# A message-passing kernel: every value product in the second pass, stores on SyncE, the two gathers in turn

## Chip, cores, metric

The kernel runs on 1 core of a Trainium2 chip. The metric is device time in microseconds of one execution. Three timed runs of the kernel before gave a median of 889.56 us (888.55 to 889.84).

## What is computed

A graph layer on N = 625 nodes and E = 20000 edges of F = 256 features, followed by a mixture-of-experts layer. Only the graph layer is touched by the change. Cut to what matters:

```
h    = concat([x[dst], x[src], edge_attr], axis=1)          # x layer-normalised, 20000 x 768
gate = sigmoid(bn(silu(h @ W1f + b1f) @ W2f + b2f))          # bn: mean and variance over all edges
msg  = gate * (silu(h @ W1m + b1m) @ W2m + b2m)
agg  = segment_sum(msg, dst, 625)                            # dst is sorted
x    = x + relu(x_ln + bn(agg)); then x + mixture_of_experts(layernorm(x))
```

`silu(h @ W1m + b1m)` is called the hidden value below, its product with W2m the value product, and `silu(h @ W1f + b1f) @ W2f` the gate product.

## The kernel before

The work is cut into stages that follow one another. Matrix products are done in three passes of rounded parts: each operand is split into a high part (`hi`, rounded) and the remainder (`lo`), and hi x hi, hi x lo and lo x hi are summed (`PASSES`). A product of two 128-row blocks of depth and 512 edges is thus six matmuls, and one of 256 x 256 with 512 edges is twelve.

**Setup (0 to about 36 us).** The node part of the first layer is computed once per node, into two tables in memory, `table_dst` and `table_src`, of 625 rows of 512 numbers each. SyncE stores them in pieces (L182, L187).

**Edge pass (to about 542 us).** Edges are taken in 40 groups of 512 (the last has 32), four groups (`b` = 0 to 3) to a turn of a hardware loop; group g is 4i + b. The batch normalisation of the gate needs statistics over all edges, so the gate can't be applied yet: the pass writes two intermediate arrays to memory, `z_gate` (gate product) and `h_val`. For each group:
- GpSimd gathers rows of the two tables by indirect DMA, four transfers of 128 rows for `dst` into `pre` (L122) and four for `src` into `from_src` (L404). There are four buffers; those of group g are free when TensorE has done group g-4 (`h1_psum`). VectorE adds the two (L512).
- SyncE loads the edge features `ea` (L117), TensorE transposes them (L555), ScalarE rounds (L417), VectorE makes the remainder (L488).
- TensorE does the first layer in four column blocks of six matmuls (L568), and adds the rows from `pre` by four transposing matmuls each (L577). Blocks 0 and 1 belong to the gate, 2 and 3 to the hidden value.
- ScalarE applies SiLU to the gate blocks twice (rounded, L450, and full, L451); VectorE makes the remainder (L531); TensorE does the gate product (L604), ScalarE copies it (L425) and issues the store of `z_gate` (L429), and VectorE takes its statistics (L494).
- Odd groups: ScalarE applies SiLU to the hidden value (L469) and issues its store to `h_val` (L433).
- Even groups: ScalarE makes the hidden value twice (L468, L469), VectorE its remainder (L525), TensorE the value product in the middle of the next, odd group's step (`value_layer`, L589), ScalarE adds the bias (L461) and issues the store of the finished value to `h_val` (L437).

**Message pass (about 542 to 734 us).** Per group the arrays are loaded again by SyncE (L319, L322; four buffers), ScalarE applies the sigmoid (L716), the message is gate times value, TensorE transposes it (L849), ScalarE rounds (L728), VectorE makes the remainder (L799), and TensorE adds it to the nodes by products with a one-hot matrix (L863), one window of 125 nodes at a time. VectorE makes the one-hot matrix of the next group with one operation for each window that the group touches (L791); which windows those are is read from a table, and the others are branched over.
- Even groups: `h_val` holds the finished value, and GpSimd makes the message for both halves in one operation (L692).
- Odd groups: `h_val` holds the hidden value. ScalarE rounds it (`hidden_hi`, L328), GpSimd makes the remainder (`split_hidden`, L332), TensorE does the value product (`second_layer`, L834), its half 0 one step before its half 1, and VectorE makes the message with the bias (L780). There are two message buffers.

**The rest (about 734 to 890 us)** is batch normalisation of the sums and the expert layer.

The order on each engine is written out by hand; engines meet only at semaphores, and a wait holds up everything that stands behind it on its engine.

## Time and profile before

The profiled execution took 891.85 us; its span from the first to the last instruction was 890.0 us, with a mean granted TensorE clock of 0.954. The page of the profile gives the busy time of each engine over that span:

| engine | busy us | share | instructions |
|---|---|---|---|
| TensorE (PE) matmuls | 801.7 | 90% | 4536 |
| TensorE (PEld) weight loads | 680.6 | 76% | 4537 |
| VectorE (DVE) | 538.2 | 60% | 883 |
| ScalarE (ACT) | 477.9 | 54% | 855 |
| GpSimd (POOL) | 451.4 | 51% | 391 |
| DMA | 226 GB/s over the span | | 67756 packets |

Matmuls are pipelined, so their durations overlap and the start of one to the start of the next is what it costs. An indirect DMA on GpSimd is counted as busy while its list of transfers is written.

### The profile page before, as it was taken

What the parts mean: (1) busy time and instruction counts of PE and PEld (TensorE: products, weight loads), DVE (VectorE), ACT (ScalarE), POOL (GpSimd) and SP (SyncE); (2) the same over time, 40 slices, a digit from 0 to 9 for tenths busy, and PEclk for the clock granted to TensorE, in tenths of its full rate; (3) what the DMA queues carried; (4) which work ended last, traced back from release to release, by engine and by line L of the source; (5) the groups of instructions that cost most, each with busy time, mean ns of one, the idle gap of its engine ahead of it and who ended that gap; (6) DMA issues with size and microseconds to landing.
All of it is one profiled execution on the core that took longest, in us unless ns stands there. A gap on an engine that the chain in (4) does not pass through costs nothing. (4 is left out here: it accounts for less than half of the span.)

```text
span 890.0 us, 14611 instructions
## 1 busy us (share of the span) xinstructions
PE 801.7 (90%) x4536; PEld 680.6 (76%) x4537; DVE 538.2 (60%) x883; ACT 477.9 (54%) x855; POOL 451.4 (51%) x391
## 2 busy tenths in 40 slices
PE   4579999999999999999999997888779874799998
PEld 3468888888888888888888885666667662799998
DVE  5257655566655555565665543888787874666664
ACT  4135555555555555555555555666557661565661
POOL 2578777666766667666666103556455573100000
PEclk9779999999999999999999996999999995699999
DMA  7778899888888878888889823676575733001201
GB/s 210 238 246 295 290 321 328 317 304 303 295 289 304 297 274 298 297 306 305 302 280 325 328 94 154 227 256 216 184 260 197 265 132 108 1 25 51 91 24 30
DMA packets 67756, 201.74 MB, mean 227 GB/s; under 512 B 10912, under 2 KB 18878, under 8 KB 67726
## 3 DMA queue, kind: packets, MB, share of 16 engines
q0 software_dynamic: 25024, 81.94, 28.3%
q1 hardware_dynamic: 31182, 77.48, 24.8%
q10 hardware_dynamic: 11520, 41.95, 12.3%
q8 instruction: 16, 0.26, 0.1%
q14 instruction: 14, 0.11, 0.0%
HBM read 156.19 MB, written 45.14 MB: 226 GB/s over the span
## 5 line engine op out<-in xcount | busy, mean ns | idle before, releaser
L122 POOL DMA_INDIRECT pre<-table_dst,idx x157 | 159.9, 1019 | 108.2 <-PE p_h L577 56.5
L404 POOL DMA_INDIRECT from_src<-table_src,idx x157 | 162.0, 1032 | 47.9 <-issue 47.9
L568 PE MATMUL p_h<-eaT_hi,w_hi 128*128 128x512 f32 (+1 forms) x320 | 134.4, 420 | 1.7 <-DVE eaT_lo L488 1.7
L568 PE MATMUL p_h<-eaT_lo,w_hi 128*128 128x512 f32 (+1 forms) x320 | 126.2, 394 | 0.0
L568 PE MATMUL p_h<-eaT_hi,w_lo 128*128 128x512 f32 (+1 forms) x320 | 125.8, 393 | 0.0
L494 DVE BATCH_NORM_STATS2 gate_stats<-zg_st 128x512 f32 (+2 forms) x80 | 54.3, 681 | 105.1 <-ACT zg_st L425 104.7
L531 DVE TENSOR_TENSOR h_lo<-h_full,h_hi 128x512 fp32r<-128x512 f32 (+1 forms) x80 | 54.5, 681 | 103.8 <-ACT h_full L451 103.5
L512 DVE TENSOR_TENSOR pre<-pre,from_src 128x512 f32<-128x512 f32 (+1 forms) x157 | 98.6, 688 | 11.9 <-DMA from_src<-table_src,idx 11.9
L577 PE MATMUL p_h<-ident,pre 128*128 128x128 f32 x628 | 95.4, 274 | 11.4 <-DVE pre L512 11.4
L577 PEld LDWEIGHTS p_h<-ident,pre 128*128 128x128 f32 x628 | 78.5, 141 | 33.8 <-DVE pre L512 12.1
L450 ACT ACTIVATE h_hi<-p_h 128x512 fp32r<-128x512 f32 (+1 forms) x80 | 47.1, 588 | 94.9 <-PE p_h L577 94.9
L692 POOL TENSOR_TENSOR msgT<-hv,gate 128x1024 f32<-128x1024 f32 x20 | 47.7, 2385 | 78.4 <-ACT gate L716 78.4
L863 PEld LDWEIGHTS p_agg<-msg,onehot 128*125 128x125 f32 x346 | 45.3, 193 | 46.1 <-DVE msg L799 45.8
L863 PE MATMUL p_agg<-msg,onehot 128*125 128x256 f32 x346 | 53.0, 299 | 30.1 <-DVE msg L799 30.1
L332 POOL TENSOR_TENSOR hvT_lo<-hv,hvT_hi 128x1024 fp32r<-128x1024 f32 x20 | 54.6, 2731 | 46.5 <-ACT hvT_hi L328 46.5
L791 DVE TENSOR_TENSOR onehot<-node_id,idx_num 128x500 fp32r<-128x500 f32 (+1 forms) x44 | 70.5, 1609 | 7.5 <-issue 6.9
L425 ACT COPY zg_st<-p_z 128x512 f32<-128x512 f32 (+1 forms) x80 | 46.1, 578 | 52.6 <-PE p_z L604 52.6
L469 ACT ACTIVATE hv_st<-p_h 128x512 f32<-128x512 f32 (+1 forms) x80 | 46.8, 586 | 46.2 <-PE p_h L577 46.1
L568 PEld LDWEIGHTS p_h<-eaT_hi,w_lo 128*128 128x128 f32 x320 | 60.6, 189 | 13.9
L568 PEld LDWEIGHTS p_h<-eaT_hi,w_hi 128*128 128x128 f32 x320 | 60.8, 190 | 11.8 <-issue 1.9
L568 PEld LDWEIGHTS p_h<-eaT_lo,w_hi 128*128 128x128 f32 x320 | 61.2, 191 | 9.3
L728 ACT CAST msg<-p_msg 128x512 fp32r<-128x512 f32 (+1 forms) x80 | 42.5, 580 | 48.2 <-PE p_msg L849 48.2
(213 smaller groups left out, 1876.9 us busy)
## 6 DMA issues: line engine op xcount, KB each, us to landing
z_gate<-zg_st ACTq DMA_DIRECT2D x40, 512.0 KB, 4.4
h_val<-hv_st ACTq DMA_DIRECT2D x40, 512.0 KB, 6.0
hv<-h_val SPq DMA_DIRECT2D x40, 512.0 KB, 5.5
gate<-z_gate SPq DMA_DIRECT2D x40, 512.0 KB, 4.6
ea<-in_edge_attr_dram SPq DMA_DIRECT2D x39, 512.0 KB, 6.9
raw<-in_L_ffn_W_dram SPq DMA_DIRECT2D x16, 512.0 KB, 4.6
pre<-table_dst,idx POOLq DMA_INDIRECT x157, 4.0
from_src<-table_src,idx POOLq DMA_INDIRECT x157, 5.8
```

What stands on the lines that cost most here:

```text
L122: pool.indirect_dma_start(pre[b][0:n, t, :], None, table_dst, bass.IndirectOffsetOnAxis(ap=idx[b][0:n, t:t + 1], axis=0)).then_inc(got_dst ...
L332: nc.gpsimd.tensor_tensor(hvT_hl[b // 2][1][:], hv[b][:], hvT_hl[b // 2][0][:], ALU.subtract).then_inc(hv_lo, 1)
L404: pool.indirect_dma_start(from_src[b][0:n, t, :], None, table_src, bass.IndirectOffsetOnAxis(ap=idx[b][0:n, T + t:T + t + 1], axis=0)).the ...
L450: nc.scalar.activation(h_hl[0][:, k, 0:w], p_h1[k][:, 0:w], ACT.Silu)
L494: nc.vector.bn_stats(gate_stats[:, j, bass.ds(g * 6, 6)], zg_st[par][:, j, 0:w]).then_inc(zg_stats, 1)
L512: nc.vector.tensor_tensor(pre[b][0:n, t, :], pre[b][0:n, t, :], from_src[b][0:n, t, :], ALU.add).then_inc(summed_ok, 1)
L531: nc.vector.tensor_tensor(h_hl[1][:, k, 0:w], h_full[k][:, 0:w], h_hl[0][:, k, 0:w], ALU.subtract).then_inc(h_lo_ok, 1)
L568: nc.tensor.matmul(p_h1[c][:, 0:w], w1_hl[wp][:, k, c * P:(c + 1) * P], eaT_hl[b % 2][dp][:, k, 0:w], start=n == 0, stop=False)
L577: last = nc.tensor.matmul(p_h1[c][:, t * TE:t * TE + n], pre[b][0:n, t, c * P:(c + 1) * P], ident[0:n, 0:n], start=False, stop=t == len(ro ...
L692: nc.gpsimd.tensor_tensor(msgT[0][:], hv[b][:], gate[b][:], ALU.mult).then_inc(msgT_even, 1)
L791: nc.vector.tensor_tensor(onehot[par][0:rows, 0:nt, n * TP:(n + 1) * TP], ids, dsts, ALU.is_equal)
L863: nc.tensor.matmul(p_agg[n // 2][:, n % 2, :], onehot[b % 2][0:rows, t, n * TP:(n + 1) * TP], msg[0:rows, part, t, :], start=False, stop=F ...
```

## The change

- `value_layer`, the second SiLU of even groups (L468), the remainder L525, the biased copy L461 and their semaphores go from the edge pass. `h_val` holds the hidden value for every group.
- The stores of `z_gate` and `h_val` are issued by SyncE, in the same queue as the loads of `ea`, instead of by ScalarE.
- Setup issues destination gathers for group 0 only; from then on each step of GpSimd issues the destination gathers of a group and then its source gathers. Before, setup issued destination gathers for groups 0 and 1, and groups 0 and 1 had only their source gathers in the loop.
- In the message pass every group is treated as the odd ones were: ScalarE `hidden_hi` and GpSimd `split_hidden` two groups ahead, TensorE the whole value product of the next group after the transposes of this one, VectorE both halves of the message. GpSimd's `message` goes, there is one message buffer, the sigmoid is done one group ahead instead of two, and VectorE makes the one-hot matrix after the two half messages.

```diff
@@ setup, GpSimd
-                    for b in range(2):
-                        gather_dst(pool, b)
+                    gather_dst(pool, 0)
@@ both passes
-            nc.scalar.copy(hvT_hl[b // 2][0][:], hv[b][:]).then_inc(hv_hi, 1)
+            nc.scalar.copy(hvT_hl[b % 2][0][:], hv[b][:]).then_inc(hv_hi, 1)
@@ edge pass, SyncE
+                    def store_gates(i, b, g):
+                        sp.wait_ge(zg_copied, KF * g + KF)
+                        sp.dma_start(z_gate[g], zg_st[b % 2][:]).then_inc(zg_stored[b % 2], 16)
+
                     def step(i, b, first=False, last=False):
                         g = 4 * i + b
                         if not (last and b >= 2):
                             sp.wait_ge(eaT_psum, KF * g + KF)
                             load_ea(sp, g + 2, b % 2, last and b == 1)
+                        if not (first and b == 0):
+                            store_gates(i, b + 1, g - 1)
+                        sp.wait_ge(hv_ok, KF * g + KF)
+                        sp.dma_start(h_val[g], hv_st[b % 2][:]).then_inc(hv_stored[b % 2], 16)
@@ edge pass, GpSimd
-                        if not (first and b < 2):
+                        if not (first and b == 0):
...
-                    for b in (1, 3):
-                        split_hidden(pool, 0, b)
+                    for b in range(2):
+                        split_hidden(pool, b, b)
@@ edge pass, ScalarE
-                        if not (first and b == 0):
-                            store_gates(g - 1, (b + 1) % 2)
-                            if b % 2 == 0:
-                                store_hidden(g - 1)
...
-                        if b % 2:
-                            for j in range(KF):
-                                act.wait_ge(v_made, KF * (2 * i + b // 2) + j + 1)
-                                nc.scalar.activation(hv_st[0][:, j, :], p_z[j][:, 0:G], ACT.Identity,
-                                                     bias=vecs[:, 3, j:j + 1]).then_inc(v_copied, 1)
...
-                            if b % 2 == 0:
-                                nc.scalar.activation(hvT_hl[1][0][:, k, :], p_h1[KF + k][:, 0:G], ACT.Silu)
@@ edge pass, VectorE
-                        if b % 2:
-                            for k in range(KF):
-                                dve.wait_ge(hv_ok, KF * g - KF + k + 1)
-                                nc.vector.tensor_tensor(hvT_hl[1][1][:, k, :], hv_st[0][:, k, :],
-                                                        hvT_hl[1][0][:, k, :], ALU.subtract).then_inc(value_lo, 1)
@@ edge pass, TensorE
-                            if c == KF and b % 2:
-                                value_layer(g - 1, 2 * i + b // 2)
@@ message pass, SyncE
-                            g, done = 4 * i + b, 2 * i + b // 2 - 1
...
+                            g = 4 * i + b
+                            sp.wait_ge(hv_lo, g - 3)
+                            load_hidden(sp, g, b)
+                            sp.wait_ge(msgT_ok, KF * (g - 3))
                             load_gates(sp, g, b)
@@ message pass, GpSimd
-                        if b % 2 and not (last and b == 3):
-                            message(i + (b == 3), (b + 1) % 4)
-                        if b % 2 and not last:
-                            split_hidden(pool, i + 1, b)
+                        if not (last and b >= 2):
+                            split_hidden(pool, 4 * i + b + 2, (b + 2) % 4)
@@ message pass, ScalarE
-                        if b % 2 and not last:
-                            act.wait_ge(v_psum, KF * (2 * i + b // 2) + KF)
-                            hidden_hi(act, i + 1, b)
+                        if not (last and b >= 2):
+                            act.wait_ge(v_psum, KF * (g + 1))
+                            hidden_hi(act, i + (b >= 2), (b + 2) % 4)
...
-                        if not (last and b >= 2):
-                            sigmoid(i + (b >= 2), (b + 2) % 4)
+                        if not (last and b == 3):
+                            sigmoid(i + (b == 3), (b + 1) % 4)
@@ message pass, VectorE
-                            if b % 2 == 0:
-                                message(1, i, b + 1, LAST if last and b == 2 else G)
+                            for j in range(KF):
+                                message(j, g + 1, (b + 1) % 4, LAST if last and b == 2 else G)
                             if last and b == 2:
                                 one_hot(g + 1, (b + 1) % 2, LAST, 1)
                             else:
                                 one_hot(g + 1, (b + 1) % 2)
-                            if b % 2:
-                                message(0, i + (b == 3), (b + 2) % 4, LAST if last else G)
@@ message pass, TensorE
+                    def second_layer(g, par, w=G):
+                        pe.wait_ge(hv_lo, g + 1)
+                        for j in range(KF):
+                            n = 0
+                            for k in range(KF):
+                                for wp, dp in PASSES:
+                                    last = nc.tensor.matmul(p_v[j][:, 0:w], w2v_hl[wp][:, k, j * P:(j + 1) * P],
+                                                            hvT_hl[par][dp][:, k, 0:w], start=n == 0, stop=n == 5)
+                                    n += 1
+                            last.then_inc(v_psum, 1)
...
-                        if b % 2 == 0:
-                            second_layer(1, i, b + 1, LAST if last and b == 2 else G)
-                        elif not (last and b == 3):
-                            second_layer(0, i + (b == 3), (b + 2) % 4, LAST if last else G)
+                        if not (last and b == 3):
+                            second_layer(g + 1, (b + 1) % 2, LAST if last and b == 2 else G)
```

## Rows read from the trace of the kernel before

**Rows 1.** Stretches: window, length; busy us (count) by engine; clock; DMA share; GB/s.

```profile
120.00:145.00 25.00, 25.00 (x135) 20.85 (x134) 14.54 (x25) 13.55 (x25) 19.21 (x20) 1.00 0.94 333
300.00:400.00 100.00, 100.00 (x536) 83.43 (x535) 57.26 (x97) 53.98 (x96) 65.64 (x66) 1.00 0.85 296
...
600.00:700.00 100.00, 82.10 (x489) 66.33 (x487) 80.83 (x89) 63.70 (x97) 55.63 (x22) 0.97 0.61 219
```

**Rows 2.** Timeline, TensorE, edge pass: start, duration, operation [idle before].

```profile
307.10 0.47 PE L604 MATMUL p_z<-h_hi,w2g_hi 128*128 128x512 f32 x1
...
320.89 0.48 PE L604 MATMUL p_z<-h_hi,w2g_hi 128*128 128x512 f32 x1
...
331.86 0.47 PE L604 MATMUL p_z<-h_hi,w2g_hi 128*128 128x512 f32 x1
```

**Rows 3.** Groups by line: busy us, mean ns; idle before them and its releaser.

```profile
L863 PE MATMUL p_agg<-msg,onehot 128*125 128x256 f32 x346 | 53.0, 299 | 30.1 <-DVE msg L799 30.1
```

**Rows 4.** Timeline, GpSimd, edge pass.

```profile
70.34 3.11 POOL L122 DMA_INDIRECT pre<-table_dst,idx  x1 [0.30 <-issue]
...
305.91 1.36 POOL L404 DMA_INDIRECT from_src<-table_src,idx  x1 [0.30 <-issue]
...
308.14 0.94 POOL L122 DMA_INDIRECT pre<-table_dst,idx  x1 [0.86 <-PE p_h L577]
```

**Rows 5.** DMA issues: count, KB each, median us to landing.

```profile
ea<-in_edge_attr_dram SPq DMA_DIRECT2D x39, 512.0 KB, 6.9
```

**Rows 6.** Timeline, start of the edge pass.

```profile
23.84 1.80 SPq L182 DMA_DIRECT2D table_dst<-rows_dst  x3
...
26.17 6.33 SPq L187 DMA_DIRECT2D table_src<-rows_src  x10
...
28.01 1.17 POOL L122 DMA_INDIRECT pre<-table_dst,idx  x1 [8.68 <-DMA table_dst<-rows_dst]
...
38.25 0.95 POOL L404 DMA_INDIRECT from_src<-table_src,idx  x1 [0.30 <-issue]
...
50.08 1.12 PE L577 MATMUL p_h<-ident,pre 128*128 128x128 f32 x4 [11.36 <-DVE pre L512]
```

**Rows 7.** Timeline, one group of the message pass.

```profile
625.08 1.09 PE L849 MATMUL p_msg<-ident,msgT 128*128 128x128 f32 x8 [0.47 <-issue]
...
625.92 0.48 PE L834 MATMUL p_v<-hvT_hi,w2v_hi 128*128 128x512 f32 x1
...
626.39 1.29 DVE L799 TENSOR_TENSOR msg<-p_msg,msg 128x512 fp32r<-128x512 f32 x2 [0.77 <-ACT msg L728]
...
627.17 0.40 PE L834 MATMUL p_v<-hvT_hi,w2v_lo 128*128 128x512 f32 x1
...
627.73 1.21 PE L863 MATMUL p_agg<-msg,onehot 128*125 128x256 f32 x8 [0.16 <-DVE msg L799]
628.28 1.05 ACT L328 CAST hvT_hi<-hv 128x1024 fp32r<-128x1024 f32 x1
...
628.43 0.75 DVE L780 SCALAR_TENSOR_TENSOR msgT<-p_v,vecs,gate 128x512 f32<-128x512 f32 x1 [0.76 <-ACT gate L716]
...
629.01 1.09 PE L849 MATMUL p_msg<-ident,msgT 128*128 128x128 f32 x8
```

**Rows 8.** Timeline, one-hot operations with and without GpSimd beside them.

```profile
561.71 0.68 DVE L791 TENSOR_TENSOR onehot<-node_id,idx_num 128x500 fp32r<-128x500 f32 x1 [0.53 <-issue]
...
592.74 2.38 POOL L692 TENSOR_TENSOR msgT<-hv,gate 128x1024 f32<-128x1024 f32 x1 [4.01 <-ACT gate L716]
...
593.50 2.15 DVE L791 TENSOR_TENSOR onehot<-node_id,idx_num 128x500 fp32r<-128x500 f32 x1
```

**Rows 9.** Groups by line.

```profile
L332 POOL TENSOR_TENSOR hvT_lo<-hv,hvT_hi 128x1024 fp32r<-128x1024 f32 x20 | 54.6, 2731 | 46.5 <-ACT hvT_hi L328 46.5
```

**Rows 10.** Timeline, first and last transposes of the message pass.

```profile
551.64 0.66 PE L849 MATMUL p_msg<-ident,msgT 128*128 128x128 f32 x2 [2.00 <-POOL msgT L692]
...
730.99 0.38 PE L849 MATMUL p_msg<-ident,msgT 128*32 128x128 f32 x2
```

More of the change, by code:

```diff
@@ L580, in add_rows, with second_layer @@
                         last.then_inc(h1_psum, 1)
-                    def value_layer(g, m):
-                        pe.wait_ge(value_lo, KF * m + KF)
-                        for j in range(KF):
-                            pe.wait_ge(zg_copied, KF * g + j + 1)
-                            n = 0
-                            for k in range(KF):
-                                for wp, dp in PASSES:
-                                    last = nc.tensor.matmul(p_z[j][:, 0:G], w2v_hl[wp][:, k, j * P:(j + 1) * P],
-                                                            hvT_hl[1][dp][:, k, :], start=n == 0, stop=n == 5)
-                                    n += 1
-                            last.then_inc(v_made, 1)
-                    def second_layer(g, i, b, w, first=False):
+                    def second_layer(g, w, first=False):
                         pe.wait_ge(h_lo_ok, KF * g + KF)
                         for j in range(KF):
-                            if b % 2:
-                                pe.wait_ge(v_copied, KF * (2 * i + b // 2) + j + 1)
-                            elif not first:
+                            if not first:
                                 pe.wait_ge(zg_copied, KF * g - KF + j + 1)
@@ L616, in step @@
                                 transpose_ea(g + 1, i + (b == 3), (b + 1) % 4, last and b == 2)
[L617 to L618 removed]
                             first_layer(g, b, c, first and b == 0, w)
                             add_rows(g, b, c, short)
[L621 removed]
+                        second_layer(g, w, first and b == 0)
                     transpose_ea(0, 0, 0)
@@ L645, in gnn_moe @@
             tmp = sb(s, "tmp", [P, 4, KF])
-            msgT = [sb(s, f"msgT{b}", [P, KF, G]) for b in range(2)]
+            msgT = sb(s, "msgT", [P, KF, G])
             msg = sb(s, "msg", [TE, 2, T, F], F32R)
@@ L706, in step @@
                                                     ALU.subtract).then_inc(w2e_lo, 1)
-                    message(0, 0, first=True)
                     groups(pool, step)
@@ L742, in _ @@
                     act.wait_ge(bn_ok, 1)
-                    for b in range(2):
-                        sigmoid(0, b)
+                    sigmoid(0, 0)
                     groups(act, step)
@@ L816, in _ @@
                     dve.load(flags, active[:, 0:NT])
+                    for j in range(KF):
+                        message(j, 0, 0)
                     one_hot(0, 0)
-                    message(0, 0, 1)
                     groups(dve, step)
```

80 lines of the change are left out of this document (19 added, 61 removed).

## The prediction, made before the result was known

> **What bounds the kernel now.** I read the busy times of the page first, then the stretches by stage, because the stages of this kernel have different limits. In the edge pass (about 49 to 540 us) TensorE is busy for all of every stretch at full granted clock, while VectorE, ScalarE and GpSimd are busy 54 to 77% [rows 1]. The starts of the gate product give its rhythm: from an even group's to the next odd group's 13.79 us, from an odd one's to the next even one's 10.97 us [rows 2]; 19 long steps and 18 short ones repeat this within 0.01. Only the value product of the even groups (L589, twelve products) makes the difference of 2.82 us, and TensorE never waits inside either step. In the message pass (551.6 to 731.0) TensorE is busy 82% and VectorE 81% [rows 1], and TensorE's matmuls idle 30.1 us for `msg` from VectorE [rows 3]. So the change takes work out of a stage in which TensorE is the bound and puts it into one in which TensorE has room. After the message pass nothing changes.
>
> **Edge pass, the value products leave.** Twenty products of 2.82 us stood on the bound engine: 20 x 2.82 = 56.4 us. The last of them (in the short group) stood on the path too. With them go, per pair of groups, ScalarE's two extra SiLUs, two copies with bias and all stores' issue, and VectorE's two subtractions; both engines idle over 40% of the stage [rows 1], so I cost these at nothing (both ends: 0 to -1 us, for a copy that TensorE might have met late).
>
> The gain is only there if the rows that TensorE adds arrive every 10.97 us. Two suppliers have to be asked. GpSimd issues eight gathers a group; one takes 0.94 and 0.30 to the next, so 10.0 us, plus about 0.4 where one begins inside a VectorE operation (1.36) [rows 4]. In the 10.97 steps of before it does its eight and then still waits for TensorE (idle 0.86 of which 0.30 is the usual gap) [rows 4], so 10.97 is met with 0.56 us to spare. The DMA engines: the stretch 300 to 400 moves 296 GB/s at share 0.85 with 12.38 us a group, that is 10.5 us of transfers and 3.66 MB a group; at 10.97 it is share 0.96 and 334 GB/s. The stretch 120 to 145 ran at 0.94 and 333 GB/s with TensorE still fully busy [rows 1]. So the new rhythm needs just what the chip has shown for 25 us. Gathers run up to four groups ahead, so a late one costs nothing unless the mean rate falls short. I take the full 56.4 and keep +0 to +21 us (11.5 us a group) as the loss if the mean falls short.
>
> SP's queue gets the stores. In order it now waits for the transpose of group g, loads the edge rows of g+2, waits for the gate copy of g-1, stores it, waits for the SiLU of g, stores that. The load of g+2 is therefore queued behind the SiLU of g-1, about half a group later than now; it is needed in the middle of group g+1, some 18 us on, for a transfer of 6.9 us [rows 5]. Free. The stores sit behind nothing longer than a group, and their buffers are needed two groups later. Free; if they were not, ScalarE would stall and TensorE a group after it.
>
> **Start, gathers in turn.** Now eight destination gathers are issued from 28.01 to 38.0 and the first source gather is at 38.25; TensorE, idle 11.36 us, begins to add at 50.08 [rows 6]. Afterwards the source gathers of group 0 come after four destination gathers, at 33.0, but not before the source table is stored: SP issues its last store at about 32.5 [rows 6], and the destination table was there 2.4 us after its last issue (25.64 to 28.01), so about 34.9. That is 3.3 us earlier, and the whole pass follows. Against this, group 1 loses its head start of four destination gathers (5 us), so the first groups are gathered only just ahead of their use; and early in the pass three gathers met VectorE's additions and took over 3 us instead of 0.94, the first of them 3.11 [rows 4]; each takes 2.2 us or more from GpSimd, and if they recur TensorE waits 1 to 5 us. I take -2 (ends -3.3 and +2).
>
> **Message pass.** One group before has 8 transposes, 6 products, 8 aggregation products; afterwards 12 products in every group. I add TensorE's part from one group: transposes from 625.08, products from 0.84 later, the sixth beginning 1.25 after the first, aggregation 627.73 to the next transposes 629.01 = 1.28 [rows 7]. The first product of a row of them takes 0.31, the others 0.23, so twelve take 2.88, and a group 0.84 + 2.88 + 1.28 = 5.0 us. The partners, counted from the start T of the transposes: VectorE's subtractions T+1.31 to T+2.60 (VectorE then makes half 0 of the next message, its product and sigmoid being there at T+2.6) [rows 7], so the aggregation no longer waits: TensorE reaches it at T+3.7. Half 1 of the message (0.75) starts when the twelfth product is through, T+3.9, ends T+4.7, just before the next transposes at T+5.0. VectorE's one-hot (0.67) follows at T+4.6. On this loop TensorE is the bound, 5.0 us, against 4.60 now ((730.99-551.64)/39) [rows 10]. The hand-over gaps of TensorE vary (0.47 before 625.08 [rows 7]), so I take 5.2 (ends 5.0 and 5.65).
>
> GpSimd's product (2.39) is replaced by a second split (2.4 to 2.8) [rows 8, 9]: 0 on TensorE's loop, since a split is ready two groups before it is used, but it holds off VectorE's one-hot. Alone a one-hot takes 0.68; started inside GpSimd's operation it ended 0.53 after that operation did, 2.15 in all [rows 8]. Afterwards the split of group g+3 starts when ScalarE's copy (1.05) is done, and that copy and the last half message (0.75) are released by the same product. So the one-hot begins at T+4.6 and the split at T+5.05: VectorE is first by 0.4 us. The Trainium skill (SBUF — State Buffer, section "SBUF: two separate sides") says that GpSimd and a VectorE operation with two SBUF inputs take a shared port as an exclusive lock, whichever starts first keeping it for its whole instruction; by that rule the forecast has no such stall with one one-hot, and the rival below has one in each group.
>
> Groups whose edges span two windows need a second one-hot, which comes behind the split: 346 aggregation products are 43 windows of 8 and 2 for the short group, so 4 such groups in 39 [rows 3]. Each costs about 2.5 us (1.05 more products and 1.4 of blocking). Sum: 39 x 5.2 + 10 = 213 against 179.4 now, +33.4 us. The first message is made by VectorE when ScalarE's sigmoid ends, not by GpSimd, for which TensorE idled 2.00 [rows 10]: -1.5 (ends 0 and -2). Loads in this pass are issued three groups ahead and the traffic a microsecond falls, so nothing is added for them.
>
> **Sum.** -56.4 - 2 + 33.4 - 1.5 = -26.5 us. The profiled execution has span 890.0 and time 891.85; the median of the three runs, 889.56, is 2.3 below that time, and I apply the difference to it: 889.56 - 26.5 = 863 us.
>
> **Rivals.**
> (a) Gathers or DMA bind the edge pass. For: the needed share of 0.96 is above every long stretch, and collisions with VectorE stretch gathers. Against: the spare 0.56 us in each short step, a collision costing only 0.45 in the loop. At 11.5 us a group, +21: 884. It becomes slower than before only above 11.6 us.
> (b) The one-hot loses its race every second group. Then its end moves from T+5.3 to about T+8.0, the next subtractions and aggregation start about 1.1 us late, and the group after that recovers: 5.65 a group, +17.5: 880.
> (c) The other side: the one-hot loses the race in every group. Then each group is a serial chain on VectorE and GpSimd: split 2.4, one-hot 0.5 after it, subtractions 1.3, two half messages 1.5, hand-over 0.5 = 6.2 us a group, +39 us: 902, slower. The point from which it decides is 5.2 + 26.5/39 = 5.9 us a group. For: the present pass does show one-hots blocked behind GpSimd [rows 8]. Against: now GpSimd starts before the half message ends (592.74 against 593.50) [rows 8], afterwards it waits for ScalarE; and if the one-hot is late, TensorE's 5.0 lets it catch up.
> (d) No extra costs: 5.0 a group and only 6 us for double windows, start -3.3: 850.
>
> **Chances.** Forecast 0.62 (its own range 855 to 872), (a) 0.15, (b) 0.11, (c) 0.05, (d) 0.07. The range for 8 in 10 takes (b) and most of (a) in and leaves (c): 851 to 884. This kernel's measurement tells about 0.2% (1.8 us) from no change. Faster: all but (c) and a worse (a): 0.92; within 0.2%: 0.02; slower: 0.06.
>
> **What would show it.** The starts of the gate product should be 10.97 apart in all full groups and the edge pass should end near 482; a larger step with TensorE waiting for `pre` from VectorE is (a). TensorE's first addition should be near 47. In the message pass the transposes should be 5.0 to 5.4 apart and one-hots about 0.7; one-hots of 2 us with steps over 5.6 are (b) or (c). The span from the end of the aggregation on must be the same 156 us. The prediction is wrong if the message pass grows by more than the edge pass shrinks, or if TensorE shows waits in the edge pass after its first group.

## The result, and the profile after

The changed kernel takes 841.71 us (median of 4 runs, 838.58 to 842.62) against 889.05 (4 runs, 887.97 to 889.84): ratio 0.946, interval 0.943 to 0.949. It is faster, as forecast, but by 47 us and not by 26.5; 841.7 lies below the range of 851 to 884. The profiled execution is the fastest of the four, 3 us below their median (span 836.4, time 838.58), and that of before lies 2.8 us above its own, so the spans differ by 53.6 us where the medians differ by 47.3.

The stretches of the edge pass and of the message pass, to be laid beside [rows 1]:

```profile
120.00:145.00 25.00, 25.00 (x137) 20.91 (x137) 15.15 (x26) 12.93 (x24) 19.52 (x19) 1.00 0.97 338
300.00:400.00 100.00, 100.00 (x547) 83.72 (x546) 60.96 (x102) 49.97 (x91) 77.77 (x74) 1.00 0.96 335
540.00:640.00 100.00, 97.39 (x595) 85.37 (x594) 78.64 (x106) 72.22 (x102) 51.31 (x22) 1.00 0.61 215
```

TensorE is still busy all the time in the edge pass, and the DMA engines carry 335 GB/s at share 0.96 for as long as the pass lasts. In the message pass TensorE went from 82% to 97% busy: it is the bound there now. The starts of the gate product [rows 2] and the group of aggregation products [rows 3]:

```profile
310.04 0.47 PE L564 MATMUL p_z<-h_hi,w2g_hi 128*128 128x512 f32 x1
...
321.01 0.47 PE L564 MATMUL p_z<-h_hi,w2g_hi 128*128 128x512 f32 x1
```

```profile
L801 PE MATMUL p_agg<-msg,onehot 128*125 128x256 f32 x346 | 48.2, 283 | 5.9 <-DVE msg L743 4.1 <-issue 1.9
```

The steps of the edge pass are 10.97 us, but for two (11.51 and 11.84, near 72 and 105 us), in which TensorE waits 0.31 and 0.64 us for `pre`, and the last two (10.55, as before, and 6.55 for the step to the short group). The aggregation's idle time before it fell from 30.1 to 5.9 us. The start of the edge pass [rows 6] shows what taking the gathers in turn did:

```profile
27.06 6.36 SPq L187 DMA_DIRECT2D table_src<-rows_src  x10
28.91 1.17 POOL L122 DMA_INDIRECT pre<-table_dst,idx  x1 [9.94 <-DMA table_dst<-rows_dst]
...
38.14 0.95 POOL L411 DMA_INDIRECT from_src<-table_src,idx  x1 [4.29 <-DMA table_src<-rows_src]
...
45.51 2.54 DVE L491 TENSOR_TENSOR pre<-pre,from_src 128x512 f32<-128x512 f32 x4 [8.23 <-DMA from_src<-table_src,idx]
...
48.10 1.12 PE L551 MATMUL p_h<-ident,pre 128*128 128x128 f32 x4 [7.78 <-DVE pre L491]
```

The first source gather starts at 38.14, as before (38.25), not at 34.9: it waits 4.29 us for the stores of the source table, which land 4.7 us after the last of them was issued (33.42). Still the first addition of TensorE comes 2 us earlier (48.10 for 50.08): the first four source gathers land in 3.5 to 4.0 us, where they took 5.0 to 6.1.

What paces GpSimd in the edge pass changed too. Its waits before its gathers from 100 to 450 us, before and after:

```profile
POOL pre L122 <- PE p_h L577: 48.1, 22, 3.7
```

```profile
POOL pre L122 <- issue: 39.3, 129, 0.3
POOL from_src L411 <- issue: 39.0, 128, 0.3
```

Before, GpSimd waited 48.1 us for buffers that TensorE had yet to free. After, it never idles more than its usual 0.30 us: one gather takes 1.06 us on average, eight with their gaps 10.95 us, beside TensorE's 10.97. The last gather of a group landed 22 to 28 us ahead of TensorE's first addition (from the 13th group on); now, after the first eight groups, it lands 4 to 6 us ahead, and VectorE's additions need 2.5 of these.

One group of the message pass, to be laid beside [rows 7]:

```profile
532.66 0.67 DVE L735 TENSOR_TENSOR onehot<-node_id,idx_num 128x500 fp32r<-128x500 f32 x1
532.68 1.04 PE L789 MATMUL p_msg<-ident,msgT 128*128 128x128 f32 x8
533.07 2.55 POOL L331 TENSOR_TENSOR hvT_lo<-hv,hvT_hi 128x1024 fp32r<-128x1024 f32 x1 [2.12 <-ACT hvT_hi L326]
533.32 1.08 ACT L672 CAST msg<-p_msg 128x512 fp32r<-128x512 f32 x2 [0.33 <-PE p_msg L789]
533.47 0.47 PE L778 MATMUL p_v<-hvT_hi,w2v_hi 128*128 128x512 f32 x1
...
533.94 1.29 DVE L743 TENSOR_TENSOR msg<-p_msg,msg 128x512 fp32r<-128x512 f32 x2 [0.60 <-ACT msg L672]
...
535.95 1.41 DVE L724 SCALAR_TENSOR_TENSOR msgT<-p_v,vecs,gate 128x512 f32<-128x512 f32 x2 [0.72 <-ACT gate L660]
536.12 0.40 PE L778 MATMUL p_v<-hvT_hi,w2v_lo 128*128 128x512 f32 x1
536.35 1.11 PE L801 MATMUL p_agg<-msg,onehot 128*125 128x256 f32 x8
536.64 1.05 ACT L326 CAST hvT_hi<-hv 128x1024 fp32r<-128x1024 f32 x1 [0.84 <-PE p_v L778]
537.27 0.67 DVE L735 TENSOR_TENSOR onehot<-node_id,idx_num 128x500 fp32r<-128x500 f32 x1
537.29 1.03 PE L789 MATMUL p_msg<-ident,msgT 128*128 128x128 f32 x8
537.77 2.46 POOL L331 TENSOR_TENSOR hvT_lo<-hv,hvT_hi 128x1024 fp32r<-128x1024 f32 x1 [2.16 <-ACT hvT_hi L326]
```

From transposes to transposes 537.29 - 532.68 = 4.61 us. No operation of TensorE has a wait in front of it; the aggregation begins 1.12 us after `msg` is complete (533.94 + 1.29 = 535.23). The one-hot starts 0.5 us ahead of the split (537.27, 537.77) and takes 0.67. The step before a group with edges in two windows, and that group's aggregation (16 products), in the same view:

```profile
569.54 3.48 DVE L735 TENSOR_TENSOR onehot<-node_id,idx_num 128x500 fp32r<-128x500 f32 x2
569.95 2.55 POOL L331 TENSOR_TENSOR hvT_lo<-hv,hvT_hi 128x1024 fp32r<-128x1024 f32 x1 [2.11 <-ACT hvT_hi L326]
...
572.95 1.27 DVE L743 TENSOR_TENSOR msg<-p_msg,msg 128x512 fp32r<-128x512 f32 x2
...
574.28 2.15 PE L801 MATMUL p_agg<-msg,onehot 128*125 128x256 f32 x16 [0.89 <-DVE msg L743]
574.64 2.42 POOL L331 TENSOR_TENSOR hvT_lo<-hv,hvT_hi 128x1024 fp32r<-128x1024 f32 x1 [2.15 <-ACT hvT_hi L326]
575.46 2.13 DVE L735 TENSOR_TENSOR onehot<-node_id,idx_num 128x500 fp32r<-128x500 f32 x1
```

The first of the two one-hots (569.54) is ahead of the split, the second is caught behind it: both together take 3.48 us, the subtractions come late and TensorE waits 0.89 us. The one-hot of the group that follows (575.46, 2.13 us) is behind its split too, which costs nothing there.

The 39 steps of the pass are 33 of 4.60 to 4.63, a first of 4.79, four of 6.65 to 6.79 (two windows) and a last of 3.86.

**Balance of the span** (before, after, difference):

| piece, by TensorE's starts | before | after | difference |
|---|---|---|---|
| to the first gate product | 59.4 | 56.2 | -3.2 |
| first to last gate product | 479.5 | 424.5 | -55.0 |
| to the first transposes | 12.7 | 10.3 | -2.5 |
| first to last transposes | 179.35 | 187.7 | +8.35 |
| to the end | 159.0 | 157.7 | -1.3 |
| sum | 890.0 | 836.4 | -53.6 |

### The profile page after: what moved, and what is told of

It is laid out like the page before. It is cut to its first block and busy times, and to the rows that moved or that the text cites. A ratio compares the mean times of both kernels' runs of the same rounds, so it can differ in the third digit from the quotient of the medians.

```text
span 836.4 us, 14472 instructions
## 1 busy us (share of the span) xinstructions
PE 782.8 (94%) x4536; PEld 677.1 (81%) x4537; DVE 520.4 (62%) x883; ACT 450.8 (54%) x795; POOL 457.2 (55%) x391
## 5 line engine op out<-in xcount | busy, mean ns | idle before, releaser
L122 POOL DMA_INDIRECT pre<-table_dst,idx x157 | 173.6, 1106 | 57.5 <-issue 47.5
L411 POOL DMA_INDIRECT from_src<-table_src,idx x157 | 156.0, 994 | 51.8 <-issue 46.6
L331 POOL TENSOR_TENSOR hvT_lo<-hv,hvT_hi 128x1024 fp32r<-128x1024 f32 x40 | 100.2, 2506 | 114.6 <-ACT hvT_hi L326 114.6
L542 PE MATMUL p_h<-eaT_hi,w_hi 128*128 128x512 f32 (+1 forms) x320 | 136.3, 426 | 1.5 <-DVE eaT_lo L467 1.5
L551 PEld LDWEIGHTS p_h<-ident,pre 128*128 128x128 f32 x628 | 77.9, 140 | 31.3 <-DVE pre L491 10.3
L724 DVE SCALAR_TENSOR_TENSOR msgT<-p_v,vecs,gate 128x512 f32<-128x512 f32 (+1 forms) x80 | 56.6, 735 | 23.8 <-ACT gate L660 15.1
L778 PE MATMUL p_v<-hvT_hi,w2v_hi 128*128 128x512 f32 (+1 forms) x160 | 66.6, 417 | 1.4 <-POOL hvT_lo L331 1.4
L564 PE MATMUL p_z<-h_hi,w2g_hi 128*128 128x512 f32 (+1 forms) x160 | 66.0, 412 | 0.0
L778 PE MATMUL p_v<-hvT_lo,w2v_hi 128*128 128x512 f32 (+1 forms) x160 | 63.3, 395 | 0.0
L778 PE MATMUL p_v<-hvT_hi,w2v_lo 128*128 128x512 f32 (+1 forms) x160 | 63.2, 395 | 0.0
```

Source lines behind the costliest of these rows:

```text
L122: pool.indirect_dma_start(pre[b][0:n, t, :], None, table_dst, bass.IndirectOffsetOnAxis(ap=idx[b][0:n, t:t + 1], axis=0)).then_inc(got_dst ...
L331: nc.gpsimd.tensor_tensor(hvT_hl[b % 2][1][:], hv[b][:], hvT_hl[b % 2][0][:], ALU.subtract).then_inc(hv_lo, 1)
L411: pool.indirect_dma_start(from_src[b][0:n, t, :], None, table_src, bass.IndirectOffsetOnAxis(ap=idx[b][0:n, T + t:T + t + 1], axis=0)).the ...
L542: nc.tensor.matmul(p_h1[c][:, 0:w], w1_hl[wp][:, k, c * P:(c + 1) * P], eaT_hl[b % 2][dp][:, k, 0:w], start=n == 0, stop=False)
L551: last = nc.tensor.matmul(p_h1[c][:, t * TE:t * TE + n], pre[b][0:n, t, c * P:(c + 1) * P], ident[0:n, 0:n], start=False, stop=t == len(ro ...
L564: last = nc.tensor.matmul(p_z[j][:, 0:w], w2g_hl[wp][:, k, j * P:(j + 1) * P], h_hl[dp][:, k, 0:w], start=n == 0, stop=n == 5)
```

## Experiments

The theory after the comparison: TensorE alone sets both passes; the message pass costs 8 us and not 33 because its own work there is 4.61 us a group, and the lock between GpSimd and VectorE costs only in the four groups with two windows. The rivals: the gathers or the DMA engines set something in the edge pass; GpSimd's split, or the one-hot behind it, is part of the 4.61; the turn-taking and the moved stores are worth much by themselves.

**The kernel after once more**, on the chip of the first experiments.

> The changed kernel as it is, timed on the same chip as the two variants below so that they can be compared with it. Expected 841 us, ratio to the kernel before 0.946.

Measured 841.74 (5 runs, 837.41 to 842.49; before 890.5), ratio 0.943, interval 0.941 to 0.946. The steps of the message pass repeat to 0.02; in the edge pass the late steps are 11.28 and 11.07 this time. A third set beside the last experiment, with this on record:

> The kernel after once more, to stand beside the halved split on the same chip: 841 to 842, steps 4.61 and 6.7 in the message pass, one or two late steps in the edge pass.

gave 840.68 (6 runs, 838.5 to 841.95; before 890.15).

**Gathers as before.** Only the turn-taking from the first group on is undone:

```
-                    gather_dst(pool, 0)
+                    for b in range(2):
+                        gather_dst(pool, b)
...
-                        if not (first and b == 0):
+                        if not (first and b < 2):
```

> The changed kernel with the gather order of before (destination gathers of groups 0 and 1 in setup). Theory A (the turn-taking order is worth what my start term said): the first source gather is issued at the same time as now, about 38.2 us, because it waits for the source table in either order, but lands about 2 us later behind four more gathers, so TensorE's first addition comes at about 50 instead of 48 us; against it the two late steps of the gate product at the start (11.51 and 11.84 instead of 10.97, 1.4 us) go. Net +0.6 us, within measurement. Rival B: the order matters for the whole pass, because GpSimd's head start is lost for good: the variant is 3 us or more faster or slower, with other steps than 10.97 us.

Measured 841.76 (5 runs, 841.23 to 843.41), ratio 0.945 (0.944 to 0.946). The first gate product comes at 59.6 instead of 57.2, but the late steps are gone too: the full steps of the pass are 10.97. The transposes run from 493.5 to 681.3, 187.7 us. Not all of the 2.4 us at the start belongs to the turn-taking: in the ten traces that have it, the first gate product is anywhere from 56.2 to 59.9, as the source table lands sooner or later (the first source gather starts from 37.7 to 41.2) and the granted clock differs there. What separates the traces cleanly is the time from the first source gather to TensorE's first addition: 10.0 to 10.3 us in those ten, 10.9 in this one, 11.8 in the kernel before. So the turn-taking gains 0.6 to 0.9 us there by this run, gives part of it back in the late steps, and is worth nothing in the whole that these runs can tell.

**Stores on ScalarE.** SyncE's stores go back to ScalarE's queue, with their waits:

```
+                    def store(g, par):
+                        act.wait_ge(zg_copied, KF * g + KF)
+                        act.dma_start(z_gate[g], zg_st[par][:]).then_inc(zg_stored[par], 16)
+                        act.wait_ge(hv_ok, KF * g + KF)
+                        act.dma_start(h_val[g], hv_st[par][:]).then_inc(hv_stored[par], 16)
```

> The changed kernel with the stores of both arrays issued by ScalarE after its SiLUs, as before, and not by SyncE. Theory A (stores on SyncE are worth nothing, TensorE is the bound and ScalarE is busy half the time): 0, the steps of the gate product stay 10.97 us and the total within 2 us of the changed kernel. Rival B: with DMA at a share of 0.96 a third queue takes a share from the gathers, and the edge pass gets steps over 11 us: +0.3 us a group or more, 12 us in all.

Measured 846.78 (5 runs, 843.23 to 848.01), ratio 0.950 (0.948 to 0.952): 5 us slower than the kernel after on the same chip. The steps are 10.97 to 11.01 but for one of 12.57, and the last two full ones, 11.14 and 14.81 (the last is 10.55 elsewhere). In the two traces the gate products take 5.3 us longer, 4.3 of them in that one step. What made it is in SyncE's queue and in VectorE's wait:

```profile
453.55 0.45 SPq L321 DMA_DIRECT2D hv<-h_val  x1
454.05 0.49 SPq L318 DMA_DIRECT2D gate<-z_gate  x1
454.58 0.50 SPq L321 DMA_DIRECT2D hv<-h_val  x1
455.12 0.49 SPq L318 DMA_DIRECT2D gate<-z_gate  x1
...
472.02 2.50 DVE L491 TENSOR_TENSOR pre<-pre,from_src 128x512 f32<-128x512 f32 x4 [5.58 <-DMA from_src<-table_src,idx]
```

Without stores to wait for, SyncE issues the first loads of the message pass for two groups within 1.6 us, while the last gathers are under way. The gathers issued from 454.66 on then take 9.5 to 11.8 us to land instead of 8.4 to 10.0, the last of them is issued only at 462.6, and VectorE waits 5.58 us for the last group. In the rerun of the kernel after the same loads stand behind a group's stores, one pair at 453.96 and the next at 464.93, and its last gather is issued at 457.0. From 440 to 465 us the DMA engines move 406 GB/s here, 360 there. So the move to SyncE does gain something, but not by relieving ScalarE: the stores meter SyncE's other loads. That they do it in this way is read from one trace; I have not tried the loads alone at other places.

**A longer way to the one-hot.** A memset of 128x1024 goes ahead of the one-hot on VectorE, so that GpSimd's split would start first:

```
                                 message(j, g + 1, (b + 1) % 4, LAST if last and b == 2 else G)
+                            nc.vector.memset(pad[b % 2][:], 0.0)
```

> The changed kernel with one extra VectorE operation in each group of the message pass, a memset of 128 x 1024 numbers that nothing reads, between the two half messages and the one-hot operation. It takes about 1 us. Theory A (exclusive sharing with GpSimd; the one-hot wins a race by 0.4 us now): the one-hot now begins behind GpSimd's split and waits for its end, 2 us instead of 0.67; the next remainder and aggregation come late in every second group, and the mean step of the transposes grows from 4.6 to 5.3 or 5.4 us, +25 to +30 us in all. Rival B (no race, VectorE simply has room: 1.29 + 1.41 + 0.67 + 1.0 = 4.4 us of work in a step of 4.61): steps stay 4.61 and the total is unchanged within 3 us.

Measured 848.22 (2 runs), ratio 0.952. The expected loss did not come: the steps with one window stayed at 4.61 us (but for one of 5.78 and the last, 5.27), those with two went from 6.7 to between 7.7 and 8.1. The timeline says why:

```profile
561.34 0.91 DVE L752 MEMSET pad<- 128x1024 f32 x1 [0.16 <-issue]
561.50 3.56 POOL L331 TENSOR_TENSOR hvT_lo<-hv,hvT_hi 128x1024 fp32r<-128x1024 f32 x1 [1.05 <-ACT hvT_hi L326]
...
562.17 0.61 DVE L736 TENSOR_TENSOR onehot<-node_id,idx_num 128x500 fp32r<-128x500 f32 x1
```

The split was released inside the memset, and now the split is the one that is long: 3.32 us on average instead of 2.51, while the one-hot behind the memset took 0.61. It ends at 565.06, 2.28 us after the one-hot is through (562.78), about the length of a split alone, and every split that is released inside a memset ends 2.27 to 2.29 us after the one-hot behind that memset. So GpSimd was held through the memset and on through the one-hot. The experiment did not do what it was made for, and it says nothing of a late one-hot.

**Eight value products in the message pass** instead of twelve (those with the remainder of the weights are left out):

```
-                                for wp, dp in PASSES:
+                                for wp, dp in PASSES[:2]:
```

> The changed kernel with 8 instead of 12 value products per group in the message pass: the pass of rounded hidden value times remainder of the weights is left out, so the output is less exact. Theory A (TensorE is the bound of the message pass of the changed kernel, at its pipelined rate): the step falls by up to 4 x 0.233 = 0.93 us, from 4.61 to 3.7; ScalarE then has 3.66 us of work in it and may hold it at 3.8 to 3.9; total -28 to -36 us. Rival B (VectorE and GpSimd set the step, as in the pass of the kernel before): the step stays at 4.6 and the total within 3 us.

Measured 846.23 (2 runs), ratio 0.950: slower than the kernel after by 5 us, with 0.9 us less work for TensorE in each group; neither theory had that. The steps alternate, mostly 4.1 to 4.4 and 5.2 to 5.6, 191.1 us in all. The one-hot loses its race:

```profile
560.59 1.23 PE L801 MATMUL p_agg<-msg,onehot 128*125 128x256 f32 x8 [1.08 <-DVE msg L743]
560.76 2.42 POOL L331 TENSOR_TENSOR hvT_lo<-hv,hvT_hi 128x1024 fp32r<-128x1024 f32 x1 [1.95 <-ACT hvT_hi L326]
561.74 1.09 PE L789 MATMUL p_msg<-ident,msgT 128*128 128x128 f32 x8
561.78 1.93 DVE L735 TENSOR_TENSOR onehot<-node_id,idx_num 128x500 fp32r<-128x500 f32 x1
...
566.39 2.49 DVE L735 TENSOR_TENSOR onehot<-node_id,idx_num 128x500 fp32r<-128x500 f32 x1
```

With products that end earlier, ScalarE's copy and GpSimd's split come ahead of the one-hot (560.76 for 561.78), and the one-hot takes 2.00 us on average instead of 1.00. It is over 1.2 us in 38 of 44 cases: it loses in nearly every group, as rival (c) of the prediction had it, and every second step makes up part of the loss, as (b) had it. VectorE is then busy 172 of 180 us and makes TensorE wait for `msg` (24.7 us in 25 waits).

**The same with a short split**: GpSimd's split of that kernel is cut to 16 columns from the third group on.

```
-            nc.gpsimd.tensor_tensor(hvT_hl[b % 2][1][:], hv[b][:], hvT_hl[b % 2][0][:],
+            nc.gpsimd.tensor_tensor(hvT_hl[b % 2][1][:, :, 0:w], hv[b][:, :, 0:w], hvT_hl[b % 2][0][:, :, 0:w],
```

> As the version with 8 value products in the message pass, and GpSimd's split of the hidden values (2.4 us for 1024 columns) cut to 16 columns from the third group on; the rest of the columns of hvT_lo are old values. If the one-hot comparison of that version is slow (mean 2.00 us against 1.00 in the kernel after) because GpSimd's two-input operation holds what VectorE's needs, it falls to 0.7 us, and the steps lose their alternation (4.4 and 5.2 us, 4.9 on average) for about 3.7 to 4.0: the message pass is 35 to 45 us shorter than there, the whole about 805 to 812. If VectorE's own work or the transfers of hv and gate bind, the one-hot falls but the steps stay at 4.4 to 4.9: 835 to 846.

Measured 820.37 (2 runs), ratio 0.922. The pair of runs shows the lock: nothing of VectorE's own work was changed, and its one-hot fell from 2.00 to 0.75 us, the pass from 191.1 to 169.2 us, the time by 25.9.

```profile
L735 DVE TENSOR_TENSOR onehot<-node_id,idx_num 128x500 fp32r<-128x500 f32 (+1 forms) x44 | 32.7, 751 | 0.1
```

The steps became mostly 3.9 to 4.4, on average a little longer than the 3.7 to 4.0 expected, and the time is 8 us above the upper end that I had written. TensorE now waits for `msgT`, in chain with ScalarE's sigmoid (ScalarE is busy 83% there).

**Short split alone, all twelve products.**

> The kernel after with GpSimd's split cut to 16 columns from the third group on (the rest of hvT_lo are old values), all products kept. If TensorE alone sets the steps with one window, they stay at 4.61; those with two windows fall from 6.7 to about 5.4 (4.61 and six or seven more products at 0.12), the last step too: 834 to 837. If the split were part of the 4.61, the steps would fall below 4.5 and the time below 832.

Measured 838.11 (2 runs), ratio 0.942. The steps with one window stay at 4.60 to 4.63: GpSimd is no part of them, TensorE alone sets them. Those with two windows fall from 6.7 to between 5.54 and 5.58. The last step rose from 3.86 to 5.54, and with it the time stays 1 us above the expected range: without the long splits GpSimd reaches its next work, the splits of the expert weights, earlier, and one of these catches the last full one-hot.

```profile
671.51 2.37 POOL L650 TENSOR_TENSOR w2e_lo<-raw,w2e_hi 128x1024 fp32r<-128x1024 f32 x1 [0.86 <-ACT w2e_hi L681]
...
672.48 1.94 DVE L735 TENSOR_TENSOR onehot<-node_id,idx_num 128x500 fp32r<-128x500 f32 x1 [0.49 <-issue]
```

TensorE then waits 1.39 us for `msg`, and the granted clock falls to the lower of its two levels (1.2 GHz) at 675.6, under the last aggregation.

**Eight gate products in the edge pass**, by the same edit at L564 (part of the gate's product is left out), to see how near the next bound is.

> The changed kernel with 8 instead of 12 gate products per group in the edge pass: the pass with the remainder of the weights is left out, so the output is less exact. TensorE then needs 10.97 - 0.93 = 10.04 us a group. Theory A (DMA is the next bound, just below TensorE's: share 0.96 at 10.97, so 10.5 us a group at full share): the mean step of the gate product falls only to 10.5 to 10.7 us, TensorE waits for the added rows; total -12 to -18 us. Rival B (the DMA share is no bound, gathers have room): steps of 10.04 us, total -36 us. Rival C (GpSimd's issue is the next bound, 8 x 1.25 plus collisions): steps of 10.2 to 10.5 us with GpSimd issuing without a break, -20 to -30 us.

Measured 821.87 (2 runs), ratio 0.922: 20 us less than the kernel after, where four products less in 40 groups are 37 us of TensorE. The message pass is the same (187.7 us). The gate products' steps spread from 10.04 to 11.95 and average 10.5. The stretches show TensorE no longer filled, and the DMA engines near a full share:

```profile
200.00:300.00 100.00, 99.41 (x552) 82.43 (x551) 61.69 (x106) 54.59 (x100) 76.42 (x78) 1.00 0.99 357
300.00:400.00 100.00, 96.03 (x534) 79.33 (x533) 61.13 (x106) 52.11 (x95) 76.62 (x77) 1.00 0.98 349
```

VectorE waits 75.1 us for `from_src` in 34 waits from 100 to 450 us. So the supply of rows binds 0.5 us below the 10.97 of the kernel after. Rival (a) was near, but on the other side of the line. Which part of the supply it is, the run leaves open. The loss of 20 us and the mean of 10.5 lie where theories A and C meet: the DMA share is 0.98 to 0.99, as in A, and GpSimd issues without a break (262 gathers with 0.30 us between them, 10.4 us for eight), as in C.

**The kernel before with a short message on GpSimd**: its product for the even groups is cut to 16 columns.

```
-                        nc.gpsimd.tensor_tensor(msgT[0][:], hv[b][:], gate[b][:], ALU.mult)
+                        nc.gpsimd.tensor_tensor(msgT[0][:, :, 0:w], hv[b][:, :, 0:w], gate[b][:, :, 0:w], ALU.mult)
```

> The kernel before with GpSimd's product for the messages of even groups cut to 8 of 512 columns (after the first group), so that the sums are wrong; nothing else is changed. Theory A (the message pass of the kernel before is bound by VectorE's one-hots waiting behind two GpSimd operations back to back, not by TensorE, whose pipelined need is 2 x 0.79 + 12 x 0.233 + 0.16 + 2 x 0.94 = 6.4 us a pair): the mean of a pair of steps falls from 9.2 to 7 to 8 us, -24 to -44 us in all. Rival B (the pass is bound by TensorE or by the chain of transposes, rounding, remainder and aggregation): the pair stays within 0.3 of 9.2, total within 6 us.

Measured 884.2 (3 runs, 880.82 to 885.74; before 890.78), ratio 0.993, interval 0.987 to 0.998. The one-hots fell from 1.61 to 0.71 us, 39 us in sum, but the time by only 6.6, between the two theories: a pair of TensorE's steps takes 8.7 us on average instead of 9.2. TensorE still waits 20.6 us for `msg` (28.3 before). One thing in the way is ScalarE's wait for `hv`, 20.2 us in 13 waits (16.0 in 15 before):

```profile
646.42 1.05 ACT L328 CAST hvT_hi<-hv 128x1024 fp32r<-128x1024 f32 x1 [2.38 <-DMA hv<-h_val]
```

So the kernel before did pay for the lock in its message pass, and taking the even groups' message off GpSimd brings less than 1%.

**The split in halves.** The two-window groups still lose their second one-hot to the split. Here nothing is left out; the split is done as two operations of 128x512:

```
+            for k in range(KF):
+                nc.gpsimd.tensor_tensor(hvT_hl[b % 2][1][:, k, :], hv[b][:, k, :], hvT_hl[b % 2][0][:, k, :],
+                                        ALU.subtract).then_inc(hv_lo, 1)
...
-                            sp.wait_ge(hv_lo, g - 3)
+                            sp.wait_ge(hv_lo, KF * g - 3 * KF)
...
-                        pe.wait_ge(hv_lo, g + 1)
+                        pe.wait_ge(hv_lo, KF * g + KF)
```

> The kernel after with the split of the hidden values done as two GpSimd operations of 128x512 in place of one of 128x1024; nothing is left out. Steps with one window stay at 4.61 (TensorE binds). In the four steps with two windows the second one-hot waits for half a split instead of a whole one: 6.7 falls to about 6.0, so 838 to 840 against 841.7, and the one-hot's mean falls from 1.00 to about 0.85. If the lock does not set these steps: 841 to 842. If GpSimd pays much per operation: nothing changes either, since its split (2.5 of 4.6 us) has slack.

Measured 835.58 (6 runs, 831.61 to 838.42), ratio 0.939 (0.936 to 0.942), against 840.68 and 0.945 (0.942 to 0.948) for the kernel after, timed side by side: 5 us faster, more than the 2 to 4 us expected, and the two intervals do not overlap. The steps with one window stay at 4.61, those with two fall from 6.7 to between 5.56 and 5.69, nearly as far as with the split cut to 16 columns. The two one-hots, the split in halves beside them, and the aggregation, now without a wait:

```profile
571.61 2.37 DVE L736 TENSOR_TENSOR onehot<-node_id,idx_num 128x500 fp32r<-128x500 f32 x2
...
572.01 3.13 POOL L332 TENSOR_TENSOR hvT_lo<-hv,hvT_hi 128x512 fp32r<-128x512 f32 x2 [1.97 <-ACT hvT_hi L326]
...
575.30 2.07 PE L802 MATMUL p_agg<-msg,onehot 128*125 128x256 f32 x16
```

The second one-hot waits for one half only: 1.78 us, where it was 2.90 behind the whole split. The halves cost GpSimd 1.38 us each, 2.76 for 2.51 before, which hides in its slack. This version beats both kernels.

## Why the prediction was wrong

**The edge pass: the size right, the margin not.** -56.4 forecast, -55.0 measured. The full steps but two are 10.97, the DMA share of 0.96 and the 334 GB/s worked out from the stretches came as 0.96 and 335. The two late steps are 0.5 and 0.9 us over; by the prediction's last sentence such waits behind the first group were a sign of its being wrong, and they are too small for that to matter. What did not come is the 0.56 us that GpSimd was to have to spare in each step. I took it from steps in which GpSimd had run ahead and waited for buffers. In the kernel after it never waits for one, eight gathers take 10.95 us at 1.06 each (0.94 taken), and the rows land a few us before their use, not four groups ahead. That the step stayed at TensorE's 10.97 thus owes more to luck than the working says. The eight-product run shows that the supply can go to 10.5 a group and no further.

**The start: the size about right, the reason wrong.** I had the source gather at 34.9, taking for the source table the 2.4 us that the destination table needed; it needed 4.7 and the gather started when it did before. The gain of 2 us at the first addition is there, and 3.2 at the first gate product, so the gathers' order did not bring it in the way that I wrote. Four gathers less are issued ahead of the first source gathers, and these land in 3.5 to 4.0 us instead of 5.0 to 6.1; the run with the gathers as before puts that at under 1 us. The rest of the 3.2 us is within what the start varies between traces of the same order, so that the size came out right is luck. The run without the turn-taking has no late steps and the same time, so the term is worth about nothing in the whole.

**The stores: right that they are free on SyncE, blind to what they do there.** I asked only whether the loads behind them would be late. That they hold the next pass's loads back, to the gathers' good, showed only when they were moved away: 5 us, 4.3 of them in one step of the trace.

**The message pass: here the forecast failed.** The mechanism was right: TensorE is the bound, the one-hot is ahead of the split (by 0.5 us, forecast 0.4), it takes 0.67, and the two-window groups lose the race. The size of TensorE's loop was not: 5.2 us a group taken, 4.61 measured. Its parts:

- Transposes to the first product: 0.84 taken, 0.79 measured.
- Twelve products: 2.88 and 2.88 (536.35 - 533.47).
- Aggregation to the next transposes: 1.28 taken, 0.94 measured. This is the step that failed. I read the 1.28 from a group in which the aggregation had waited for `msg` ([rows 7] shows the wait), while the same paragraph showed that it would wait no longer. In the trace after, 34 one-window groups without a wait have 0.93 to 0.95.
- An allowance of 0.2 for hand-over gaps that "vary": there are none when nothing waits. The gap of 0.47 that I cited stood, again, in a pass in which TensorE waited each group.

Of the 0.34, 0.10 stands right behind the wait: the second product begins 0.22 to 0.23 us after the first and not 0.12, in all 34 one-window groups of before that waited. The other 0.24 stands at the far end, between the last product and the transposes:

```profile
628.66 0.28 PE L863 MATMUL p_agg<-msg,onehot 128*125 128x256 f32 x1
629.01 0.32 PE L849 MATMUL p_msg<-ident,msgT 128*128 128x128 f32 x1
...
708.64 1.21 PE L863 MATMUL p_agg<-msg,onehot 128*125 128x256 f32 x8 [1.16 <-DVE msg L799]
709.69 0.49 PE L849 MATMUL p_msg<-ident,msgT 128*128 128x128 f32 x3
```

After its aggregation TensorE's sequencer branches over the windows that stand behind the group's own (L858; the trace has three such branches in the first window's groups, of 0.20 us each at the median), and at the end of a loop turn there is the loop's branch too (L339). A wait at the aggregation holds these up as well. The waited groups of before fall apart by just that: 1.17 to 1.45 us in the first window and 1.63 to 1.77 there at the end of a turn, 1.04 to 1.05 in the second window and 1.41 to 1.42 at the end of a turn, 1.03 to 1.06 in the last two windows. The 0.47 is such an end of a turn as well. In the trace after, the branches are done before the aggregation begins (two of them at 535.81 and 536.07, ahead of 536.35). So what looked like a duration of the aggregation was a wait, and the branches that it had held up.

Together 0.05 + 0.34 + 0.20 = 0.59 a group, over 33 groups 19.5 us; the first and last steps give 1.7 more, and the two-window groups, taken at 7.7 and measured at 6.7, 4.0. That is 25 of the 27 us by which the span's change was missed; the rest is +1.4 in the edge pass and -3.5 in the start, the first message and the end.

**The rivals.** (a) did not happen, and the run with eight gate products shows where it begins. (b) and (c) did not happen here; the run with eight products in the message pass has the lost race of (c) in nearly every group and the alternating steps of (b), at 4.9 us a group. It is set off by less work for TensorE, not by more. Of (d), "no extra costs", I had priced the period at 5.0, and so even the lowest case still held the waits' 0.34 us. The range's lower end came from there. What the Trainium skill (SBUF — State Buffer, section "SBUF: two separate sides") says of a shared port as an exclusive lock agrees with these runs where both sides read two inputs: the one-hot of 2.00 us falls to 0.75 when the split is cut. The memset, which reads nothing, is no such operation, and the split waited for it all the same. By that rule the forecast had no stall with one window and one with two, and so it came.

## What to carry to other kernels

When work moves onto an engine that now has waits, build its new period from rows in which it did not wait, or from operations one by one; a stretch that begins with a wait is too long, here 1.03 to 1.77 us for 0.94, and the excess can stand at its far end, in instructions that the wait held up. The same goes for an engine's slack: what it showed while it was ahead (0.56 us) was gone when it no longer was. Where two engines race for one resource, the race is decided by whose releaser comes first, and shortening a third engine's work can lose it; a long operation cut in two makes losing it cheap. A transfer's place in a queue also sets when the ones behind it may start, and that can be worth more than the queue that it leaves.

## What was not expected of the hardware

- An aggregation of eight products takes 0.94 us to the next transposes when TensorE runs through, 1.03 to 1.06 when it had waited at its start and no branches stand behind it, and up to 1.77 when they do.
- The granted clock is 1.00 over the whole message pass after. Before, it was 0.965 over the pass: at the lower level (1.2 GHz) to 557.3 us and in two stretches of 3.4 us from 635.8 and 666.6, which make the 0.97 of 600 to 700 [rows 1]. At most 3.5% of 179 us, 6 us (an estimate), can have been lost by that, so without it the pass would have grown by 8 to 15 us; no run tells how much.
- A memset of 128x1024 on VectorE, with no input at all, delays a two-input operation of GpSimd that begins 0.16 us after it, and the one-hot queued behind the memset still goes first: 3.32 us for the split instead of 2.51 (means). Behind a half message (1.39 us from 560.46 on in the run with eight products) the queued one-hot did not go first.
- The DMA engines held 335 GB/s at share 0.96 from 100 to 450 us with all steps but one at 10.97, and moved 349 to 357 at 0.98 to 0.99 with eight gate products. With the stores on ScalarE and the loads of the next pass beside the gathers it was 406 at 1.02 (440 to 465 us), so GB/s at a full share depends on the mix.
